# A transformer tower on one core: a new order at two seams, and a hand-written place for every score maximum

## The chip, the core and the metric

The kernel runs on one NeuronCore of a Trainium2 chip. It is one program, launched once. The metric is the device time in microseconds (us): the median of three runs, and beside them one profiled execution whose trace gives every row below. The engines are TensorE (PE, with its weight loads as PEld), VectorE (DVE), ScalarE (ACT), GpSimd (POOL) and SyncE (SP, which issues DMAs). Each engine works through its own list of instructions in order, and waits on semaphores that other engines raise.

## The reference

Two sequences of 2048 tokens, width 128, pass through three layers:

```python
h = take(W.T, x) + b + positional                       # token rows, 128 wide
h = h + attn(layernorm(h))                              # 8 heads of 16, linear in the scores
h = h + ffn(layernorm(h))                               # attention of 2 heads of 64, then experts

# attn: masked q.k, normalised by its running mean and variance, no softmax
dots = where(causal_mask, 0, q @ k.T * scale)
t = dots - mean_so_far;  normed = t * rsqrt(mean_so_far(t*t) + EPS)
out = where(causal_mask, 0, normed * g + b) @ v

# ffn: softmax attention over unit q and k, then 8 experts, all used, mixed by a gate
attn = softmax(where(causal, l2(q) @ l2(k).T * scales, min))
y = (attn @ v) @ Wo
out = sum_e softmax(y @ gate_W + gate_b)[e] * (gelu(y @ W1[e] + b1[e]) @ W2[e] + b2[e])
```

## The kernel before

The tokens are cut into 16 blocks of 128 positions, each with both sequences (B = 2). All engines' orders are written out by hand, one function per engine.

**Stage A, the first attention (0 to about 222 us).** Because that attention has no softmax, it is computed as a recurrence over the blocks: a state (`sg`) is carried, and each block adds its own part. Block 0 is worked by a direct way of its own. In it VectorE makes the masked dots and their variance, GpSimd raises the variance to the power -0.5 (`coefs`, line 268), VectorE copies the new state out of PSUM (`state_out`, line 656) and GpSimd adds it up (`state_add`, line 264). Blocks 1 to 14 run in `step_a(c, nxt)`, one call for each block on each engine. In it PE does the dots of the first sequence (`dots`), sums, the dots of the second, the projections of the next block, and the products with the masked dots. Each block needs its input two steps ahead: `embed(c)` (VectorE: add the position, row statistics), `front(c)` (GpSimd: the statistics' power, lines 251 and 253), `normed(c)` (VectorE, line 648), and PE's transposes `xn_T(c)` (line 1032). For block 2 these stand between block 0 and `step_a(1)`: GpSimd's order is `coefs(0)`, `state_add(0)`, `front(2, 0)`; VectorE's is `state_out(0, 0)`, `state_out(0, 1)`, `embed(2)`, `normed(2)`; PE fills the time with `busy`, matmuls whose result nobody reads.

**The seam to stage B (about 215 to 232 us).** The last block (15) is written out without a loop, mixed with the first blocks of the next stage. PE ends its products with `project2(1)`, which projects block 1 for the second attention and waits until ScalarE has copied block 15's sums out of PSUM (`sums_out`, line 435).

**Stage B (about 232 to 278 us)** makes q, k and v of the second attention: `squares`, `sum_squares`, `l2_factors`, `unit_qk`, a chain of ScalarE, VectorE and GpSimd around PE's transposes. Some of PE's matmuls there (line 1245) also have no reader.

**Stage C, the second attention (about 278 to 486 us).** There are 8 items (4 chunks of 512 queries, 2 sequences), cut into 80 steps of 128 keys each. `plan()` makes the lists. In each step s, in this order on PE: `scores(s)`; a part of the row maxima of a later item; the values of step s - 2; the output part of an earlier item, if one is due at this step; then, where the step has two maxima, the second one. The parts of an output are five matmul groups that come 1, 2, 3, 7 and 8 steps after the step at which that item's output is due (`YAT`). A maximum is a pair of score matmuls into PSUM banks 3 and 4 (`pair_scores`) and a reduction of both by VectorE (`row_max`, line 866). As the two banks are used every time, the next pair waits until VectorE has reduced the one before:

```python
if guard:
    pe.wait_ge(*guard)          # guard = S["sm_used"], k + 1
```

`MSLOT` says which maxima stand in which step. Up to step 8 they come one or two at a time for the small items. From step 9 on a step has one or two ("a double step"). From step 36 (`CLOSE`) on, the last maximum of a step stands after the output part instead of before the values. VectorE's order in a step is: the maxima (both, when there are two), `head_out` if an item ends (lines 941 and 943: it scales the item's values and releases their banks, for which PE's first values of the next item wait), the gate's small operations, and the low halves of the exponentials that are VectorE's share (line 976). GpSimd takes the other low halves (line 384): both of a step, or one where `on_pool` gives the odd one to VectorE, which is in odd steps from 17 to 61 with one maximum.

In the kernel before, `plan()` spreads the maxima by a rule: as many in each step as the items' due steps ask for. This gives double steps at 9, 12, 15, 17, 20, 26, 31, 37 and 42.

**Stage D, the experts (about 486 to 832 us):** 64 rounds of up-projection, gelu, down-projection and weighted sum.

## Time and profile before

| | |
|---|---|
| three runs | 835.01 us median, 833.29 to 840.62 |
| profiled execution | 834.53 us; the span of its trace is 832.7 us, with 1.8 us around it |
| PE busy | 778.6 us (94%) |
| DVE busy | 703.0 us (84%) |
| ACT busy | 486.5 us (58%) |
| POOL busy | 337.3 us (41%) |
| mean granted clock of PE | 0.99 |

A busy share says how long an engine had an instruction in work, not that it worked at its peak: a matmul at half clock is busy twice as long. In the rows below, times count from the span's start. In a row of the timeline the brackets hold the engine's idle time before the instruction and the instruction that ended it. PE's rows are matmuls; the line 1024 is that of the helper `mm`, so they are told apart by tiles and shapes: `ps<-y,room 64x512 f32` is `dots`, `ps<-qh,kh 64x512 f16` begins `scores`, `ps<-v,room 128x65` are the values, `ps<-cst 128x512 f32` is `busy`.

### The profile page before, as it was taken

The page shows a single profiled execution, that of the slowest core. Times are in us where ns is not written, and L with a number is a line of the kernel's source. Part 1 is how long each engine was busy: PE and PEld are TensorE (multiplying, and loading weights), DVE is VectorE, ACT ScalarE, POOL GpSimd, SP SyncE. Part 2 cuts the span into 40 slices and gives each one's busy share as a digit, 9 for nine tenths or more (in the row PEclk, how much of TensorE's full clock was granted, in tenths as well). Part 3 has the DMA queues.
Part 4 walks back from the last instruction along what each step waited for, and adds up shares of the span by engine and source line. Part 5 has one row for each costly group of instructions (what it writes and reads, how often), then busy time and mean ns, then how long its engine had stood idle before and what let it go on. Part 6 is the DMA issues. An engine that isn't in the chain of part 4 may idle for free.

```text
span 832.7 us, 21068 instructions
## 1 busy us (share of the span) xinstructions
PE 778.6 (94%) x8230; PEld 552.5 (66%) x8230; DVE 703.0 (84%) x1575; ACT 486.5 (58%) x1023; POOL 337.3 (41%) x374
## 2 busy tenths in 40 slices
PE   1999999999988889998899999999999999999997
PEld 1568778877755455555556556777777777777775
DVE  3649988999688776777667999999999999999997
ACT  2435555555388667786878767455555555555553
POOL 6638999877575557665766631000000000000000
PEclk9989999999999999999999999999999999999999
DMA  4200111010000000000000000000000000000000
GB/s 132 55 10 20 39 39 27 26 27 14 1 1 1 26 2 2 3 2 2 2 2 3 2 14 2 13 2 14 2 14 2 5 11 9 7 6 11 2 15 13
DMA packets 9666, 12.09 MB, mean 15 GB/s; under 512 B 1856, under 2 KB 6592, under 8 KB 9568
## 3 DMA queue, kind: packets, MB, share of 16 engines
q1 hardware_dynamic: 8544, 8.65, 3.5%
q0 software_dynamic: 1024, 2.10, 0.9%
q8 instruction: 65, 1.06, 0.5%
q14 instruction: 33, 0.27, 0.1%
HBM read 8.65 MB, written 2.10 MB: 13 GB/s over the span
## 4 chain that ended last, share of the span: by engine, by line
PE 75%; DVE 12%; issue 5%; POOL 4%; ACT 3%; DMA 1%; DVEq 0%; ACTq 0%
PE ps L1024 74%; DVE mx L866 2%; POOL ss L345 2%; DVE room L974 2%; DVE room L976 1%; DVE qkn L820 1%; ACT room L592 1%; POOL sm L268 1%; DVE mx L861 1%; DVE ss L805 1%; DMA h_all<-emb_rows,idx 1%; DVE y L701 1%; DVE och L943 1%; PE ps L1032 0%; PE ps L1052 0%
## 5 line engine op out<-in xcount | busy, mean ns | idle before, releaser
L605 ACT ACTIVATE cst<-ps,col 128x512 f32<-128x512 f32 x256 | 175.6, 687 | 157.8 <-PE ps L1024 157.0
L1024 PEld LDWEIGHTS ps<-arena,sq 128*128 128x128 f16 x3072 | 191.9, 98 | 62.0 <-DVE sq L1005 4.9
L1024 PE MATMUL ps<-arena,sq 128*128 128x128 f16 x3072 | 213.1, 219 | 0.3 <-DVE sq L1005 0.2
L1024 PE MATMUL ps<-y,arena 128*128 128x512 f16 x768 | 207.4, 379 | 0.4 <-issue 0.4
L1005 DVE TENSOR_TENSOR sq<-cst,sq 128x512 f16<-128x512 f32 x256 | 176.3, 689 | 4.5
L384 POOL TENSOR_TENSOR room<-room 128x512 f16<-128x512 f32 (+3 forms) x122 | 123.2, 1029 | 74.8 <-ACT room L592 73.9
L999 DVE CAST sq<-cst 128x512 f16<-128x512 f32 x256 | 109.8, 429 | 7.5 <-ACT cst L605 0.5
L583 ACT ACTIVATE room<-ps 128x512 f32<-128x512 f32 (+3 forms) x160 | 76.7, 533 | 43.3 <-PE ps L1024 42.9
L866 DVE TENSOR_REDUCE mx<-ps 128x2 f32<-128x1024 f32 (+2 forms) x64 | 70.2, 1096 | 36.7 <-PE ps L1024 36.5
L1024 PEld LDWEIGHTS ps<-y,arena 128*128 128x128 f16 x768 | 64.5, 98 | 32.0 <-issue 1.2
L992 DVE SCALAR_TENSOR_TENSOR h_all<-ps,gs,h_all 128x128 f32<-128x128 f32 x256 | 77.2, 343 | 0.4 <-PE ps L1024 0.4
L1024 PEld LDWEIGHTS ps<-v,room 128*128 128x128 f16 x1632 | 55.8, 98 | 31.6 <-issue 13.8
L1024 PE MATMUL ps<-v,room 128*128 128x65 f16 (+1 forms) x1632 | 66.2, 195 | 7.7 <-DVE och L943 5.1
L592 ACT CAST room<-room 128x512 f16<-128x512 f32 (+3 forms) x142 | 72.5, 561 | 0.0
L1024 PEld LDWEIGHTS ps<-room,y 128*128 128x128 f32 x512 | 60.9, 192 | 2.7 <-ACT y L467 1.7
L1024 PE MATMUL ps<-room,y 128*128 128x34 f32 (+1 forms) x512 | 60.0, 272 | 0.5 <-ACT y L467 0.5
L268 POOL TENSOR_TENSOR sm<-sm,mhalf 128x16 f32<-128x16 f32 x15 | 43.6, 2908 | 27.5 <-DVE sm L747 22.1
L1024 PE MATMUL ps<-kh,qh 64*128 64x512 f16 (+3 forms) x160 | 33.2, 354 | 10.4 <-DVE mx L866 8.6
L752 DVE TENSOR_TENSOR y<-ps,cst 128x1024 f32<-128x1024 f32 x30 | 36.3, 1211 | 7.5 <-PE ps L1024 7.5
L976 DVE TENSOR_TENSOR room<-room 128x512 f16<-128x512 f32 (+3 forms) x38 | 36.4, 957 | 3.8 <-ACT room L592 3.1
L1024 PE MATMUL ps<-y,room 64*128 64x512 f32 x128 | 39.1, 694 | 0.0
L239 POOL DMA_INDIRECT h_all<-emb_rows,idx x32 | 31.6, 988 | 10.3 <-issue 7.9
(166 smaller groups left out, 1189.5 us busy)
## 6 DMA issues: line engine op xcount, KB each, us to landing
sq<-w_rows SPq DMA_DIRECT2D x13, 256.0 KB, 2.8
out<-h_all SPq DMA_DIRECT2D x32, 64.0 KB, 1.6
cst<-consts SPq DMA_DIRECT2D x1, 896.0 KB, 5.3
h_all<-emb_rows,idx POOLq DMA_INDIRECT x32, 2.6
hxT<-w_rows SPq DMA_DIRECT2D x2, 256.0 KB, 2.7
cst<-consts SPq DMA_DIRECT2D x1, 398.0 KB, 3.7
c<-consts SPq DMA_DIRECT2D x1, 256.0 KB, 5.2
x<-w_rows SPq DMA_DIRECT2D x1, 256.0 KB, 3.0
```

The costliest lines, as they stand in the source:

```text
L268: g.tensor_tensor(sm[:, 4], sm[:, 3], mhalf[:].rearrange("p (b h) -> p b h", b=B), ALU.pow).then_inc(S["r_ready"], 1)
L384: g.tensor_tensor(plo[:, i % PR, lo:], p32[:, i % QR, lo:], phi[:, i % PR, lo:], ALU.subtract).then_inc(S["plo_pool"], 1)
L583: a.activation(p32[:, i % QR, lo:], ps[:, i % 3, lo:], ACT.Exp).then_inc(S["s_used"], 1)
L592: a.copy(phi[:, i % PR, lo:], p32[:, i % QR, lo:]).then_inc(S["p_ready"], 1)
L605: a.activation(hid[:, f], ps[:, HBANK[f], :], ACT.Gelu_apprx_tanh, bias=col[:, K_B1 + k:K_B1 + k + 1], scale=1.0 / WS).then_inc(S["hid_rea ...
L752: v.tensor_tensor(dtm[:, b], ps[:, 3:5, :].rearrange("p z (h j) -> p (z h) j", j=P), upper.unsqueeze(1).to_broadcast([P, HA, P]), ALU.mult ...
L866: v.tensor_reduce(mx[:, it % 2, r, kb], ps[:, 3:5, 0:w], AX, ALU.max).then_inc(S["sm_used"], 1)
L976: v.tensor_tensor(plo[:, i % PR, lo:], p32[:, i % QR, lo:], phi[:, i % PR, lo:], ALU.subtract).then_inc(S["plo_dve"], 1)
L992: v.scalar_tensor_tensor(hr, ps[:, EBANK[n % 2], r * D:(r + 1) * D], gs[:, m, r, n % E:n % E + 1], hr, ALU.mult, ALU.add).then_inc(S["eo_u ...
L999: v.tensor_copy(hhi[:, f], hid[:, f]).then_inc(S["hhi_ready"], 1)
L1005: v.tensor_tensor(hlo[:, f], hid[:, f], hhi[:, f], ALU.subtract).then_inc(S["hlo_even" if f % 2 == 0 else "hlo_odd"], 1)
L1024: return t_.matmul(o, l, r, start=start, stop=stop, skip_group_check=True)
```

## The change

It does three things, and gives the maxima new steps.

1. At the end of block 0, GpSimd's order becomes `front(2, 0)`, `state_add(0)`, `coefs(0)`. VectorE's becomes `state_out(0, 0)`, `embed(2, 0)`, `state_out(0, 1)`, `normed(2, 0)`. The call `busy(1, 1)` ahead of PE's `xn_T(2)` is taken out.
2. At the seam to stage B, three matmuls of 512 columns in half precision, with no reader, are put ahead of `project2(1)`.
3. VectorE does the closing maxima of a step (the second one of a double step up to 35, and the last one from step 36 on) after `head_out` instead of before it. A function `closing(s)` counts them, for PE and VectorE alike; PE's own rule is unchanged.

The maxima follow a written list, `COUNTS`, of how many stand in each step. Their order is unchanged. The double steps from 9 on are now 9, 11, 14, 18, 20, 27, 28, 41 and 45. Each item's last maximum stays at or before its old due step. As `on_pool` looks at the number of maxima, the odd low halves of steps 17, 31 and 37 go to VectorE, and those of steps 27, 41 and 45 go to GpSimd.

```diff
--- before.py
+++ after.py
@@ -315,9 +315,9 @@
             out_bias(0)
             out_bias(1)
             gather(6, 16)
+            front(2, 0)
+            state_add(0)
             coefs(0)
-            state_add(0)
-            front(2, 0)
 
             def step_a(c, nxt, more=2, tail=True):
                 if c >= 3:
@@ -707,8 +707,10 @@
             link(v.tensor_reduce(sm[:, 1, 1], sq[:, 1], AX, ALU.add))
             dve.wait_ge(S["sq_act"], 1)
             v.tensor_scalar(sm[:, 3], sm[:, 1], inv0, DOT_EPS, ALU.mult, ALU.add).then_inc(S["var_ready"], 1)
-            for b in range(B):
-                state_out(0, b, first=True)
+            state_out(0, 0, first=True)
+            embed(2, 0)
+            state_out(0, 1, first=True)
+            normed(2, 0)
 
             def outputs(c, cur, first=False):
                 dve.wait_ge(S["coef"], c + 1 if c < NT - 1 else NT + 1)
@@ -783,8 +785,6 @@
                     normed(c + 2, cur)
                 h1_out(c - 1)
 
-            embed(2, 0)
-            normed(2, 0)
             step_a(1, 0, first=True)
             for c in range(2, NT - 2, 2):
                 for u in range(2):
@@ -951,13 +951,17 @@
                     if s == YAT[m] + DVE_Y[2]:
                         out_part(m, 5)
                 two = MSLOT.get(s, ())
-                for part in two if two and two[0][0] not in ALONE else two[:1]:
+                early = 1 if two and two[0][0] in ALONE else len(two) - closing(s)
+                for part in two[:early]:
                     row_max(*part, (0, 1))
                 if s == 1:
                     low_qk(NT - 1)
                 for it in range(len(ITEMS)):
                     if s == OAT[it]:
                         head_out(it)
+                if two and two[0][0] not in ALONE:
+                    for part in two[early:]:
+                        row_max(*part, (0, 1))
                 for m in range(LAST):
                     if s - YAT[m] in DVE_Y[:2]:
                         out_part(m, DVE_Y.index(s - YAT[m]) + 3)
@@ -1119,7 +1123,6 @@
                     at = D + h * XW + DA
                     last = mm(ps[:, 5 + b, at:at + DA], dtm[:, b, h], kv[0][:, b, h, DA:2 * DA], start=False)
                 last.then_inc(S["x_ps"], 1)
-            busy(1, 1)
             xn_T(2, 0, first=True)
 
             def step_a(c, nxt, more=True, first=False):
@@ -1220,6 +1223,8 @@
                 last.then_inc(S["x_ps"], 1)
                 if b == 0:
                     project2(0, [1])
+            for i in range(3):
+                mm(ps[:, 3, :], minus16, c16[:, 0:CH])
             project2(1)
             out_T(NT - 2)
             normed_T(2)
@@ -1421,10 +1426,10 @@
                 lone = [(*part, h) for part in MSLOT.get(s, ()) if part[0] in ALONE for h in range(HS)]
                 pairs = [part for part in MSLOT.get(s, ()) if part[0] not in ALONE]
                 assert not (lone and pairs)
-                closing = min(len(pairs), 1) if s >= CLOSE else len(pairs) // 2
+                close = closing(s)
                 for part in lone[:1]:
                     lone_scores(*part)
-                for part in pairs[:len(pairs) - closing]:
+                for part in pairs[:len(pairs) - close]:
                     pair_scores(*part)
                 if s in RAT:
                     max_row(RAT[s])
@@ -1439,13 +1444,13 @@
                 for part in lone[2:]:
                     lone_scores(*part)
                 if s < CLOSE:
-                    for part in pairs[len(pairs) - closing:]:
+                    for part in pairs[len(pairs) - close:]:
                         pair_scores(*part)
                 for m in range(LAST):
                     if s - YAT[m] in PE_Y:
                         out_part(m, PE_Y.index(s - YAT[m]) + 1)
                 if s >= CLOSE:
-                    for part in pairs[len(pairs) - closing:]:
+                    for part in pairs[len(pairs) - close:]:
                         pair_scores(*part)
 
 
@@ -1479,6 +1484,8 @@
 
 
 ALONE = (1, 2)
+COUNTS = [int(d) for d in "0222222"
+          "1121211211121211111122111111111111211121111111111111111"]
 
 
 def plan():
@@ -1493,18 +1500,12 @@
                 for r in range(4):
                     parts.append((it, r, kb, CH if kb < c else (r + 1) * P, k))
                     k += HS if it in ALONE else 1
-    due = [None, 2, 6] + [f - 3 for f in first[3:]]
-    mslot, done, credit = {}, 0, 0.0
-    for s in range(1, len(steps)):
-        left = [(sum(p[0] <= it for p in parts) - done, due[it] - s) for it in range(1, len(items)) if due[it] >= s]
-        credit += max((n / (d + 1) for n, d in left), default=0)
-        count = max([int(credit + 1e-6)] + [n - 2 * d for n, d in left])
-        for part in parts[done:done + count]:
-            mslot.setdefault(s, []).append(part)
-        done, credit = done + count, max(credit - count, 0)
+    mslot, done = {}, 0
+    for s, count in enumerate(COUNTS):
+        if count:
+            mslot[s] = parts[done:done + count]
+            done += count
     assert done == len(parts)
-    for it in range(1, len(items)):
-        assert max(s for s, ps in mslot.items() for p in ps if p[0] == it) <= due[it]
     rat = {first[it] - 1: it for it in range(1, len(items))}
     o_at = [e - 1 + LAG for e in first[1:] + [len(steps)]]
     y_at = []
@@ -1540,11 +1541,17 @@
     return {0: 1, 1: 7, 2: 5}.get(c, 0)
 
 
+def closing(s):
+    parts = [part for part in MSLOT.get(s, ()) if part[0] not in ALONE]
+    return min(len(parts), 1) if s >= CLOSE else len(parts) // 2
+
+
 def on_pool(i):
     s = i // 2
     if s >= NSTEP - 18:
         return i % 2 == 0
-    return i % 2 == 0 or len(MSLOT.get(s, ())) != 1 or s < 16 or s % 2 == 0
+    parts = len(MSLOT.get(s, ()))
+    return i % 2 == 0 or s < 16 or parts > 1 or parts == 1 and s % 2 == 0
 
 
 def rounded(i):
```

## Rows read from the trace of the kernel before

**Rows 1.** Windows: busy us (instructions) of five engines, granted clock, DMA, GB/s
```profile
45.00:59.00 14.00, 14.00 (x71) 9.90 (x72) 7.05 (x16) 4.05 (x12) 4.98 (x7) 0.76 0.00 1
216.00:232.00 16.00, 14.79 (x76) 10.04 (x75) 9.40 (x26) 5.24 (x13) 7.17 (x9) 0.89 0.00 1
400.00:490.00 90.00, 82.86 (x1316) 52.68 (x1311) 71.23 (x99) 71.34 (x149) 55.47 (x50) 0.98 0.01 2
516.00:832.00 316.00, 312.10 (x3557) 228.17 (x3554) 300.25 (x715) 160.97 (x235) 0.00 (x0) 1.00 0.03 8
```

**Rows 2.** Timeline, end of block 0: start, us, engine, line, operation
```profile
38.03 2.94 POOL L268 TENSOR_TENSOR sm<-sm,mhalf 128x16 f32<-128x16 f32 x1 [4.68 <-DVE sm L709]
...
41.11 0.43 DVE L631 TENSOR_TENSOR h_all<-h_all,cst 128x256 f32<-128x256 f32 x1
41.19 1.96 PE L1024 MATMUL ps<-room,y 128*128 128x16 f32 x16 [0.47 <-ACT y L467]
...
42.20 0.15 DVE L641 BATCH_NORM_AGGREGATE mv<-st 128x2 f32<-128x6 f32 x1
...
43.00 1.10 PE L1024 MATMUL ps<-cst 128*128 128x512 f32 x2
...
43.58 0.71 POOL L253 TENSOR_TENSOR rs<-rs,mhalf 128x2 f32<-128x2 f32 x1
...
44.98 0.69 PE L1032 MATMUL ps<-cst,room 128*128 128x128 f32 x2 [0.88 <-DVE room L648]
45.60 2.08 PE L1024 MATMUL ps<-y,room 64*128 64x512 f32 x4
...
60.16 1.13 PE L1024 MATMUL ps<-y,room 64*128 64x512 f32 x4
```

**Rows 3.** Chain that ended last: start, us; one merged piece of two consecutive blocks
```profile
59.06 3.79 PE ps L1024 x22
...
70.97 3.79 PE ps L1024 x22
```

**Rows 4.** Timeline, the seam to stage B
```profile
225.86 2.90 PE L1024 MATMUL ps<-wsm,hxT 128*128 128x384 f32 x4 [0.67 <-ACT room L435]
...
230.53 1.49 PE L1024 MATMUL ps<-wsm,hxT 128*128 128x384 f32 x4
...
232.51 1.03 PE L1024 MATMUL ps<-c 128*128 128x512 f16 x4
...
232.57 0.69 DVE L820 TENSOR_TENSOR qkn<-ps,ss 128x512 f32<-128x512 f32 x1 [0.84 <-PE ps L1201]
```

**Rows 5.** Waits in all: engine, line, for whom; us in total, times, longest
```profile
PE ps L1024 <- DVE mx L866: 8.6, 19, 1.2
...
PE ps L1024 <- DVE och L943: 5.1, 5, 1.6
```

**Rows 6.** Timeline of PE: where scores of steps 14 to 17 begin, and transposes
```profile
318.64 0.39 PE L1024 MATMUL ps<-qh,kh 64*128 64x512 f16 x2
...
320.67 0.39 PE L1024 MATMUL ps<-qh,kh 64*128 64x512 f16 x2
...
323.56 0.66 PE L1353 MATMUL ps<-cst,och 128*128 128x128 f32 x4
...
324.15 0.39 PE L1024 MATMUL ps<-qh,kh 64*128 64x512 f16 x2
...
327.23 0.34 PE L1024 MATMUL ps<-qh,kh 64*128 64x384 f16 x2
```

**Rows 7.** Timeline of PE: first values after the items' ends, steps 38, 50
```profile
385.14 0.91 PE L1024 MATMUL ps<-v,room 128*128 128x65 f16 x24 [1.62 <-DVE och L943]
...
416.41 1.15 PE L1024 MATMUL ps<-v,room 128*128 128x65 f16 x24 [1.62 <-DVE och L943]
```

**Rows 8.** Timeline of VectorE: the second maximum of step 17
```profile
330.14 1.22 DVE L866 TENSOR_REDUCE mx<-ps 128x2 f32<-128x1024 f32 x1 [0.49 <-PE ps L1024]
```

**Rows 9.** Costliest groups: busy us, mean ns, idle before
```profile
L976 DVE TENSOR_TENSOR room<-room 128x512 f16<-128x512 f32 (+3 forms) x38 | 36.4, 957 | 3.8 <-ACT room L592 3.1
```

## The prediction

> **What bounds the kernel now.** I read the windows by stage first, to see where PE is not simply at work at full clock. The experts (516 to 832 us) are: busy 312.1 of 316 us at a granted clock of 1.00 [rows 1]. The change doesn't touch them, so a gain ahead of them arrives in full at the end. Three stretches show a lower clock. From 45 to 59 us the mean is 0.76, so 0.24 x 14 / 0.5 = 6.7 us at the lower level (1.2 GHz); from 216 to 232 it is 0.89, so 3.5 us; from 400 to 490 it is 0.98, so 3.6 us [rows 1]. The first two are the change's two seams. Then I read the timeline at each seam, to see what PE waited for before the clock fell, and the chain of waits, to have the length of an undisturbed block. For the second attention I read the table of waits and PE's timeline: there PE works in steps of fixed content, so the distance between the beginnings of two `scores` is the length of a step, and what a double step costs can be read from steps of either kind.
>
> **Part 1, the end of block 0.** Before, GpSimd takes `coefs` first (its power alone is 2.94 us from 38.03), then two state additions, and ends the power of `front(2)` at 43.58 + 0.71 = 44.29. PE has done the last 16 products at 41.19 + 1.96 = 43.15, has filled 43.00 to 44.10 with `busy`, and begins the transposes of block 2 at 44.98, after 0.88 us of idleness ended by VectorE; `dots(1, 0)` begins at 45.60 [rows 2]. After, `embed` (41.11 to 42.35, 1.24 us) stands before the second `state_out`. That one ends just where `embed` begins now, at about 41.1, and waits for PE until then, so VectorE has the time. The rest is an estimate from these rows: `embed` from about 38.4 to 39.7, `front(2)` on GpSimd to about 40.7, `normed` at 41.2 behind the second `state_out`, done by 41.9. PE's own products, until 43.0, are then last, and the transposes follow at once. They took 0.69 at the lower clock, so some 0.4 at full clock: `dots(1, 0)` at about 43.4, **2.2 us earlier**. What is put back: the two state additions by about 1 us (the first begins near 40.7, still before `sums(1, 0)` asks for it near 44.6), and `coefs`, to end near 46 instead of 41.9. VectorE asks for the coefficients in `outputs(0)`, behind two masked dots, that is some 6 us after `dots(1, 0)`, near 49.5. The cover is over 3 us; without it each microsecond would cost one. `busy` costs nothing by going: PE has real work in its place.
>
> Block 1 itself: from `dots(1, 0)` at 45.60 to `dots(2, 0)` at 60.16 it lasts 14.56 us [rows 2], while two undisturbed blocks in the chain lie 70.97 - 59.06 = 11.91 us apart [rows 3]. The same `dots` took 2.08 at the lower clock and 1.13 at full [rows 2]. If PE keeps its clock through the seam, block 1 takes 11.91, and **2.65 us** come back. For this, PE no longer stands idle before the transposes, and dots and sums follow where filler and a pause stood. Sum of part 1: 4.85 us. Its bounds are 2.2 (the clock falls all the same) and 4.85.
>
> What a page says against it stands apart. The trace shows the clock of 45 to 59 us low after a stretch of narrow products, filler and a pause. The Trainium skill ("TensorE: Matmul & The Clock Gate", part 4 on PE-mode transposes) says that transposes don't count as PE being busy in the same way. The change puts transposes where filler stood, so by that rule the clock would fall all the same, which is the second rival's time below.
>
> **Part 2, three matmuls at the seam to stage B.** PE waits 0.67 us before `project2(1)`, for ScalarE's copy of the sums, and then runs its four pieces in 2.90 us, where the same four pieces of the next block take 1.49 [rows 4]. Four 512-column matmuls of the same kind as the new ones take 1.03 us together [rows 4], so three take at most 0.77: 0.67 of that fills the wait, and 0.1 is the most that shows. If they hold the clock, 1.41 comes back, and about 0.2 from the transposes behind. Who is late next: VectorE's `unit_qk(1)` waits 0.84 for PE at 232.57 [rows 4], so at least that much is PE's doing there; the chain of squares and powers also begins with `project2(1)` and moves with it. Bounds 0.8 and 1.6; I take **1.4**, as both feeders move.
>
> **Part 3, the maxima.** In all, PE waits 8.6 us for maxima and 5.1 us for `head_out` [rows 5]. The last is largest at steps 38 and 50, 1.62 us each [rows 7]: there VectorE does a maximum ahead of `head_out`, though the values that `head_out` needs are long done. With `closing`, `head_out` goes first at steps 9, 37 and 49, and both waits of 1.62 lose their cause. At step 9 PE's next pair waits for the same maximum, so nothing comes of it.
>
> Against that stand the new places. Step 14 has one maximum and no output part: 320.67 - 318.64 = 2.03 us. Step 15 has two and the transposes of an output (0.66): 324.15 - 320.67 = 3.48. Step 16 has one and a projection: 327.23 - 324.15 = 3.08 [rows 6]. So beside an output part a second maximum costs 3.48 - 2.03 - 0.66 = 0.8. Alone it must cost more: a pair and the hand-over take 0.49, the reduction 1.22 [rows 8], two rounds of that are 3.42, and 3.42 - 2.03 = 1.4. Five of the seven double steps that are given up (15, 17, 26, 31, 42) hold an output part; the seven new ones (11, 14, 18, 27, 28, 41, 45) hold none of the long ones. That costs 5 x 0.6 = 3.0 us. Some maxima in the new places are narrower, by the plan's list of parts. Scaling 1.22 by columns (an estimate), step 11 has 256 columns less than step 12 had and saves 0.6; step 28 holds one of 128 columns, saving 0.9; step 45 one of 384, saving 0.3. So the places cost 1.2 to 1.3 us. The low halves that change engine (0.96 us each on VectorE [rows 9]) are three each way: nothing in sum, up to 1 us either way by where they fall; at step 17 VectorE's comes ahead of the two maxima of step 18, which is bad.
>
> Of the two waits of 1.62 I keep the one at step 50, since no double step comes behind it. The one at step 38 is followed by the double steps 41 and 45, and at 41 VectorE also has the sum of an output part in front; I count it as given back there. So part 3 comes to 1.3 - 1.62 = **-0.3 us**. Its bounds: -3.2 (both waits, places free) and +3.
>
> **The sum.** The profiled execution took 834.53 us, 832.7 of it in the span; it is 0.5 us under the median of the three runs and inside their spread. 834.53 - 4.85 - 1.4 - 0.3 = **828.0 us**.
>
> **The rivals.** (a) The second attention gains: both waits for `head_out` go for good and the new places cost nothing. For it: 8.6 us of waits for maxima can shrink as well. Against it: the prices above. 834.53 - 6.25 - 3.24 = 825.0 us. (b) The clock falls at both seams all the same, after other instructions. Then only the 2.2 us of the earlier start and part 3 are left: 832.0 us. For it: the 16 narrow products that precede the first seam [rows 2] stay as they are. The rule on transposes above gives this time too. Against it: at the second seam the three matmuls lie exactly in the pause that precedes the fall. (c) Slower than before: a bare double step costs 1.4 us at all seven new places, while the steps that are freed keep their length, because the copies between an output's parts set them and not the maximum. 7 x 1.4 = 9.8, less 4.85 + 1.4 + 1.62 = 7.9: 836.5 us. It decides if the freed steps give back less than 1.9 us together, under 0.3 each. Against it: step 15 with two maxima is 0.8 longer than its single maximum and its transposes explain. (d) The change doesn't do what it says at the seams: GpSimd, 41% busy over all but with a chain of its own in block 1, is late next, and hardly anything arrives: 834 us.
>
> **How the numbers follow.** My forecast has a chance of 0.50, with 1.5 us either way; (a) 0.17, (b) 0.15, (c) 0.10, (d) 0.08. The range of 823 to 834 us takes in the forecast, most of (a), all of (b) and half of (d); it leaves out (c) and the ends, about 0.18. One per cent, which is about what a measurement of this kernel can tell from no change, is 8.35 us: 826.7 and 843.4. Under 826.7 lie most of (a) and a fifth to a quarter of the forecast's own spread, in sum some 0.28 to 0.30; above 843.4 only a larger (c).
>
> **What would show it.** In the changed kernel the transposes of block 2 should begin near 43.0 and `dots(2, 0)` near 55.3, and the clock from 45 to 59 us should be near 1.00. `project2(1)` should take 1.5 us, not 2.9, and the clock from 216 to 232 should be near 1.00 too. The waits for `head_out` should fall from 5.1 to about 2 us. Step 14 should be near 3.4 us, where it was 2.03, and step 15 near 2.7, where it was 3.48. I am wrong if the clock falls at another place of the same stages, if `coefs` turns out late in block 1, or if the waits for maxima grow by more than 3 us.

## The result, and the profile after

The changed kernel takes 832.68 us in the median of 22 runs (829.8 to 838.42), the kernel before, in as many runs beside it, 838.56 us (832.91 to 842.6). The ratio is 0.9947, 95% interval 0.9926 to 0.9968: 4.4 us of 838.56 (2.7 to 6.2), faster, but by less than one per cent. The forecast was 828.0 us. The time lies in the range, in the direction forecast, and 4.7 us above it. One of the six executions of a version further down, the changed kernel with its gathers spread, took 1008.01 us at a granted clock of 0.75, and its ratio leaves it out.

Two numbers of these runs matter below. The median of before is 838.56, not the 835.01 of the three runs shown; its profiled execution, 834.53, falls among the six of the 22 that lie between 832.9 and 835.1, while the other sixteen lie between 837.0 and 842.6. And the profiled execution of the changed kernel, 836.64 us with a span of 834.8, is one of its longer ones. So the two profiles show the kernels from opposite sides of their spreads, and by them alone the change would be a loss. The spread goes with TensorE's mean granted clock: the fifteen executions of the changed kernel at 0.991 or more take 829.8 to 833.83 us, the seven at 0.987 to 0.989 take 834.8 to 838.42.

The windows of the changed kernel, columns as in [rows 1], with a stretch ahead:

```profile
41.00:55.00 14.00, 14.00 (x53) 10.54 (x54) 3.01 (x6) 2.69 (x8) 5.79 (x7) 0.51 0.08 30
...
45.00:59.00 14.00, 14.00 (x58) 9.71 (x56) 6.89 (x16) 2.92 (x11) 6.33 (x8) 0.65 0.00 1
216.00:232.00 16.00, 15.08 (x94) 10.66 (x93) 10.23 (x22) 5.63 (x16) 8.06 (x10) 1.00 0.00 1
```

Against [rows 1]: the seam to stage B has full clock now (0.89 before), the first seam has less than before (0.65, was 0.76), and from 41 to 55 us TensorE worked at its lower level, 1.2 GHz, nearly throughout (0.51).

The timeline of the changed kernel, end of block 0:

```profile
31.90 0.94 PE L1028 MATMUL ps<-wqkv,room 128*128 128x128 f32 x6 [0.36 <-issue]
...
33.15 0.95 POOL L239 DMA_INDIRECT h_all<-emb_rows,idx  x1 [0.30 <-issue]
...
35.90 0.37 ACT L421 COPY room<-ps 128x256 f32<-128x256 f32 x1 [4.05 <-remote]
...
39.97 2.58 PE L1028 MATMUL ps<-room,y 128*128 128x16 f32 x16 [3.01 <-ACT y L467]
...
45.50 3.60 PE L1028 MATMUL ps<-room,y 128*128 128x16 f32 x16
48.94 0.67 PE L1036 MATMUL ps<-cst,room 128*128 128x128 f32 x2
49.53 2.08 PE L1028 MATMUL ps<-y,room 64*128 64x512 f32 x4
...
63.68 1.13 PE L1028 MATMUL ps<-y,room 64*128 64x512 f32 x4
```

and the chain of waits there, just ahead of that copy at 35.90:

```profile
31.84 4.03 another core or an unknown queue
```

Read them together. TensorE's six products for the second sample of block 1 end at 32.84. The copy on ScalarE that waits for nothing but them (line 421) begins at 35.90, 3.06 us later. The profile can't name who released it ("remote"), and the chain calls the 4 us before it an unknown queue, on a kernel of one core. Everything behind that copy is late by as much: the squares, the copy of the differences (line 467), and TensorE's narrow products at 39.97, before which it stood idle for 3.01 us. Then the clock falls, at 41.1, and stays low until 54.8. In the profile of before the same copy waited 1.02 us, and TensorE went from filler to narrow products without a pause:

```profile
33.08 0.37 ACT L421 COPY room<-ps 128x256 f32<-128x256 f32 x1 [1.02 <-PE ps L1024]
...
34.44 2.74 PE L1024 MATMUL ps<-cst 128*128 128x512 f32 x6
...
37.16 1.96 PE L1024 MATMUL ps<-room,y 128*128 128x16 f32 x16
```

The rest of the reordering is as drawn: the transposes (48.94) follow the last narrow products at once, where 0.88 us of waiting and `busy` stood [rows 2], and `dots(1, 0)` (49.53) follows the transposes.

The seam to stage B, against [rows 4]:

```profile
229.38 1.53 PE L1028 MATMUL ps<-wsm,hxT 128*128 128x384 f32 x4
...
234.72 0.69 DVE L820 TENSOR_TENSOR qkn<-ps,ss 128x512 f32<-128x512 f32 x1 [0.84 <-PE ps L1204]
```

`project2(1)` takes 1.53 us instead of 2.90 and its wait of 0.67 is filled. VectorE's wait of 0.84 stays.

TensorE's waits in all, against [rows 5]:

```profile
PE ps L1028 <- DVE mx L866: 12.9, 20, 1.6
...
PE ps L1028 <- DVE och L943: 1.3, 2, 1.1
```

`head_out` is waited for 1.3 us instead of 5.1, maxima 12.9 instead of 8.6: 14.2 in place of 13.7. And the timeline of TensorE where the scores of steps 14 to 22 begin, against [rows 6]:

```profile
319.92 0.39 PE L1028 MATMUL ps<-qh,kh 64*128 64x512 f16 x2
...
322.72 0.38 PE L1028 MATMUL ps<-qh,kh 64*128 64x512 f16 x2
...
324.21 0.39 PE L1028 MATMUL ps<-kh,qh 64*128 64x512 f16 x2 [0.46 <-DVE mx L866]
...
326.19 0.39 PE L1028 MATMUL ps<-qh,kh 64*128 64x512 f16 x2
...
329.27 0.34 PE L1028 MATMUL ps<-qh,kh 64*128 64x384 f16 x2
...
332.06 0.28 PE L1028 MATMUL ps<-qh,kh 64*128 64x256 f16 x2
...
335.45 0.39 PE L1028 MATMUL ps<-kh,qh 64*128 64x512 f16 x2 [1.60 <-DVE mx L866]
...
337.17 0.23 PE L1028 MATMUL ps<-kh,qh 64*128 64x128 f16 x2 [0.99 <-DVE mx L866]
...
338.10 0.61 PE L1028 MATMUL ps<-qh,kh 64*128 64x512 f16 x2
...
343.66 0.39 PE L1028 MATMUL ps<-qh,kh 64*128 64x512 f16 x2
```

VectorE ahead of the maxima of step 18:

```profile
333.71 0.55 DVE L980 TENSOR_TENSOR room<-room 128x384 f16<-128x384 f32 x1
334.18 1.21 DVE L866 TENSOR_REDUCE mx<-ps 128x2 f32<-128x1024 f32 x1
```

Step 14 lasts 2.80 us (was 2.03), step 15 3.47 (was 3.48), step 16 3.08 as before. Step 15 has lost a maximum and is no shorter: its one pair (324.21) waits 0.46 us for VectorE, which still has the second maximum of step 14. In the double step 18, VectorE first does step 17's low half, which GpSimd did before (0.55 us from 333.71), and reduces the first maximum from 334.18. TensorE waits 1.60 and 0.99 us for maxima, and then the product that takes 0.38 to 0.39 in the other steps takes 0.61: here too it is at the lower clock, this time in the middle of the second attention.

### The profile page after: what moved, and what is told of

The parts are those of the page before. It is cut to its first block, busy times and chain, and to the rows that moved or that the text cites. A ratio compares the mean times of both kernels' runs of the same rounds, so it can differ in the third digit from the quotient of the medians.

```text
span 834.8 us, 21070 instructions
## 1 busy us (share of the span) xinstructions
PE 779.2 (93%) x8231; PEld 553.8 (66%) x8231; DVE 703.8 (84%) x1575; ACT 487.3 (58%) x1023; POOL 337.6 (40%) x374
## 4 chain that ended last, share of the span: by engine, by line
PE 76%; DVE 12%; issue 5%; ACT 3%; POOL 3%; DMA 1%; another core or an unknown queue 0%; DVEq 0%; ACTq 0%; POOLq 0%
PE ps L1028 74%; DVE mx L866 3%; POOL ss L345 2%; DVE room L978 2%; DVE room L980 1%; DVE qkn L820 1%; DMA h_all<-emb_rows,idx 1%; ACT room L592 1%; DVE mx L861 1%; DVE ss L805 1%; PE ps L1036 0%; PE ps L1056 0%; DVE och L943 0%; POOL sm L282 0%
## 5 line engine op out<-in xcount | busy, mean ns | idle before, releaser
L1028 PEld LDWEIGHTS ps<-room,y 128*128 128x128 f32 x512 | 63.1, 198 | 5.4 <-ACT y L467 4.4
L1028 PE MATMUL ps<-room,y 128*128 128x34 f32 (+1 forms) x512 | 62.3, 277 | 3.0 <-ACT y L467 3.0
L1028 PE MATMUL ps<-kh,qh 64*128 64x512 f16 (+3 forms) x160 | 33.2, 355 | 14.7 <-DVE mx L866 12.9
```

The source lines that it names most:

```text
L1028: return t_.matmul(o, l, r, start=start, stop=stop, skip_group_check=True)
```

## The experiments

Comparisons are with the kernel before on the same chip. Its medians there were 837.17 (runs 1 to 4), 838.39 (5 to 8), 837.16 (9 to 11) and 836.03 (12).

### Each part alone

Part 1 alone, the end of block 0:

```diff
-            coefs(0)
-            state_add(0)
+            front(2, 0)
+            state_add(0)
+            coefs(0)
...
-                state_out(0, b, first=True)
+            state_out(0, 0, first=True)
+            embed(2, 0)
+            state_out(0, 1, first=True)
+            normed(2, 0)
...
-                    busy(1, 1)
```

> Part 1 alone: the new order at the end of block 0 and no filler there, everything else as before. Theory 1 (the prediction's sum): the transposes of block 2 follow PE's products without a pause, the clock holds, and the median falls by 4.85 us, to about 0.994 of before. Theory 2 (the clock falls all the same, because a stall of ScalarE earlier in block 0 leaves PE without work, as in the profile of the changed kernel, where a copy began after 4.05 us of idle time): only the earlier start is left, 2 us or less, 0.998, and the granted clock of the stretch from 45 to 59 us stays well under 1.

Measured: 834.12 us, ratio 0.9955 (0.9927 to 0.9982), so 3.8 us where T1 said 4.85 and T2 2 or less; the interval (1.5 to 6.1 us) holds both. Its profile, of the shortest of its twelve executions, 829.34 us, shows the seam at its best, with a clock of 1.00 from 45 to 59 us as T1 had it; timeline:

```profile
36.15 3.59 PE L1024 MATMUL ps<-room,y 128*128 128x16 f32 x16 [2.86 <-ACT y L467]
...
42.69 1.96 PE L1024 MATMUL ps<-room,y 128*128 128x16 f32 x16
...
44.84 1.13 PE L1024 MATMUL ps<-y,room 64*128 64x512 f32 x4
...
56.53 1.13 PE L1024 MATMUL ps<-y,room 64*128 64x512 f32 x4
```

TensorE had waited 2.86 us here too and was at the lower clock at 36.15, but it was back before the seam: the second narrow products take 1.96, and both `dots` 1.13. From the second narrow products to `dots(2, 0)` it is 56.53 - 42.69 = 13.84 us. In before it was 60.16 - 41.19 = 18.97 [rows 2], in the profile of the changed kernel 63.68 - 45.50 = 18.18. This distance contains nothing but the seam and block 1 and is the measure of part 1 from here on.

Part 2 alone, `for i in range(3): mm(ps[:, 3, :], minus16, c16[:, 0:CH])` ahead of `project2(1)`:

> Part 2 alone: the three matmuls ahead of project2(1). Theory 1: the clock from 216 to 232 us is 1.00, the four pieces of project2(1) take 1.5 us and the median falls by 1.4 us (0.998). Rival: the clock falls a little later instead, or the chain of GpSimd's powers sets the stage, and nothing is measured (1.000).

Measured: 836.86 us, ratio 0.9992 (0.9965 to 1.002): between 2.9 us and a loss of 1.7, unclear. In its profile `project2(1)` runs at full clock (1.53 us), and yet the window of 216 to 232 has 0.89 as in before; timeline and windows:

```profile
231.73 1.53 PE L1024 MATMUL ps<-wsm,hxT 128*128 128x384 f32 x4
```

```profile
216.00:232.00 16.00, 15.53 (x96) 11.99 (x95) 9.36 (x19) 5.24 (x14) 8.37 (x10) 0.89 0.00 1
```

The clock is low in an earlier part of that window, from 218.2 to 221.8 us. The rival has the fall move as well, but to a later place.

Part 3 alone, the list `COUNTS` and `closing` (the diff stands above):

> Part 3 alone: head_out before the closing maxima, and the new places. Theory 1: the second attention (scores of step 0 to scores of step 62) is 0.3 us shorter, 1.000 in the median; steps 14, 18 and 28 near 3.4 us. Rival (a) of the prediction: 3.2 us shorter, 0.996. Rival (c): some 8 us longer, 1.010.

Measured: 837.3 us, ratio 0.9994 (0.9964 to 1.0024): neither a gain nor a loss that the times can show, and not rival (c). The steps show more, in profiles that keep full clock there: from the scores of step 0 to those of step 62, TensorE takes 165.21 us with the attention of before (part 2 alone) and 165.40 with part 3 (the filler's run below), 0.2 longer. In the profile of this run it is 166.90, as the clock falls behind step 18 again. The three parts alone sum up to 3.8 + 0.7 + 0.5 = 5.0 us, near the 4.4 of all three together, but each is uncertain by 2.3 to 2.5 us, so whether they act on each other is not shown.

The seams and `head_out` first, with the old places of the maxima (the cut shows it against the changed kernel):

```diff
-COUNTS = [int(d) for d in "0222222"
-          "1121211211121211111122111111111111211121111111111111111"]
...
+    due = [None, 2, 6] + [f - 3 for f in first[3:]]
...
```

> The whole change without the new places: seams and head_out first, the double steps where they were (9, 12, 15, 17, 20, 26, 31, 37, 42). If the new places cost what the prediction says (1.3 us) and the wait for head_out at step 38 is only given back by the double steps 41 and 45, this kernel is 1.3 to 2.9 us faster than the changed one: 0.990 to 0.992 of before if the changed kernel is at 0.9947. If the new places gain, it is slower than the changed one.

Measured: 829.19 us, ratio 0.9889 (0.9857 to 0.9921), faster than the changed kernel by 0.0058 x 837 = 4.9 us. The new places cost more than the 1.3 us of the prediction, or the 2.9 if the wait at step 38 is theirs too. Timeline of TensorE, scores of steps 17 and 22:

```profile
329.71 0.34 PE L1028 MATMUL ps<-qh,kh 64*128 64x384 f16 x2
...
341.62 0.39 PE L1028 MATMUL ps<-qh,kh 64*128 64x512 f16 x2
```

Steps 17 to 21 take 341.62 - 329.71 = 11.91 us; in the changed kernel 343.66 - 329.27 = 14.39.

### What in part 3 gains and what costs

`head_out` first and nothing else, against the kernel before:

```diff
-                for part in two if two and two[0][0] not in ALONE else two[:1]:
+                early = 1 if two and two[0][0] in ALONE else len(two) - closing(s)
+                for part in two[:early]:
                     row_max(*part, (0, 1))
...
                         head_out(it)
+                if two and two[0][0] not in ALONE:
+                    for part in two[early:]:
+                        row_max(*part, (0, 1))
```

> Edit: the kernel before with head_out in front of the closing maxima alone; places and seams as before. T1 (the nine new places, not head_out, are what makes the third part worth nothing: with head_out first and the old places the trace of the earlier run was 4.36 us ahead of the kernel before between the first second-attention step and step 62, with the new places 0.09): the waits for head_out at steps 38 and 50 both go, steps 0 to 62 take about 4.3 us less than in the profile of before (1.5 of it only because the lower clock at 416.89 is gone, 2.8 without), ratio to before 0.995 to 0.9965. T2 (the prediction's: of the two waits of 1.62 one is lost later on): 1.6 us less, ratio 0.998. The maxima at 18 are at 17 here, so no granted clock under 1.00 between steps 17 and 21.

Measured: 834.68 us, ratio 0.997 (0.994 to 0.9999). Waits of TensorE:

```profile
PE ps L1028 <- DVE mx L866: 9.8, 21, 1.2
...
PE ps L1028 <- DVE och L943: 1.1, 1, 1.1
```

10.9 us in place of the 13.7 of before [rows 5]: 2.8 us less, both waits of 1.62 gone for good. That is T1 by the waits, and by the steps: 0 to 62 take 162.33 us, 2.9 less than the 165.21 of before's attention at full clock. The time, 2.5 us (0.1 to 5.0), agrees with T1 and doesn't exclude T2's 1.6.

One place put back, the second maximum of step 18 in step 17:

```diff
-          "1121211211121211111122111111111111211121111111111111111"]
+          "1121211211211211111122111111111111211121111111111111111"]
```

> Edit: the changed kernel with one of the nine places put back: the second maximum of step 18 in step 17 again. T1 (this one move is the dear one: between steps 16 and 21 the changed kernel is 2.49 us behind the old places, because the double at 18 lets TensorE wait 1.60 and 0.99 us for maxima and its clock then falls from 338.07 to 341.48): steps 16 to 21 take 2.3 to 2.8 us less than in the changed kernel, no clock under 1.00 there, ratio to before 0.9947 - 0.003 = 0.9917. T2 (every new place costs about the same, 4.3/7 = 0.6 us): 0.6 us less, ratio 0.994, and the lower clock at 338 stays.

Measured: 832.96 us, ratio 0.9937 (0.9906 to 0.9967): nearer to T2's 0.994, with T1's 0.9917 in the interval. In its profile steps 17 to 21 take 11.91 us at full clock, 2.48 less than in the changed kernel, as T1 had it; here the clock falls in steps 10 and 11 (low from 308.6 to 312.1 us). The waits for maxima fall to 11.5 us (12.9 in the changed kernel), 1.4 less, so the 2.49 us of T1 are not what the move costs each time: see the filler's run below, with the same places, where the clock did not fall in these steps.

All old places but 12, which goes to 11:

```diff
-          "1121211211121211111122111111111111211121111111111111111"]
+          "1121211121211211111211112111112111121111111111111111111"]
```

> Edit: the changed kernel with the old places except one, 12 moved to 11 as in the changed kernel. T1 (that move is the only one of the seven that gains: steps 11 and 12 take 4.57 in the changed kernel against 4.87): 0.3 us less than with all old places, ratio to before 0.9885. T2 (the 0.3 is given back at step 14, where the items' due times are): the same as with all old places, 0.989. Either way faster than the changed kernel by 4 to 5 us.

Measured: 830.36 us, ratio 0.990 (0.9857 to 0.9942). The waits of TensorE for maxima are 9.4 us here and 9.8 with all old places, and steps 0 to 62 take 161.73 us here and 162.37 there. That is T1 in the steps, by 0.6 us instead of 0.3; so small a difference the times can't show (0.990 against 0.9889).

### The late signals

Six instead of three `busy` products while TensorE waits for ScalarE in block 0:

```diff
-                    busy(1, 3)
+                    busy(1, 6)
```

> Edit: the changed kernel with six instead of three filler products (each two records of 512 columns) behind the transposes of block 0, while TensorE waits for ScalarE's copy. T1 (the clock falls at 41.11 us in the profile because TensorE stands 3.0 us idle before the narrow products, which in turn is because the signals of the products that ended at 32.83 to 34.39 us arrived only at 35.88 to 36.03): the fillers cover that wait at no cost, the granted clock of 41 to 55 us rises from 0.51 to over 0.8, the time falls by 3 to 6 us, ratio to before 0.988 to 0.991. T2 (the narrow products and transposes behind the wait bring the clock down, filler or not, and the fillers make executions without late signals 2.6 us later): clock 41 to 55 still 0.5 to 0.65, ratio 0.995 to 0.998.

Measured: 832.66 us, ratio 0.9932 (0.9906 to 0.9957). Timeline and windows:

```profile
40.63 1.96 PE L1028 MATMUL ps<-room,y 128*128 128x16 f32 x16 [1.44 <-ACT y L467]
45.45 2.19 PE L1028 MATMUL ps<-room,y 128*128 128x16 f32 x16
47.84 1.13 PE L1028 MATMUL ps<-y,room 64*128 64x512 f32 x4
...
59.53 1.13 PE L1028 MATMUL ps<-y,room 64*128 64x512 f32 x4
...
326.49 0.34 PE L1028 MATMUL ps<-qh,kh 64*128 64x384 f16 x2
...
339.70 0.39 PE L1028 MATMUL ps<-qh,kh 64*128 64x512 f16 x2
```

```profile
41.00:55.00 14.00, 14.00 (x85) 11.02 (x84) 7.25 (x21) 3.54 (x11) 8.06 (x12) 0.88 0.11 38
```

In the profile T1 comes true: the wait before the narrow products is 1.44 us instead of 3.01, the clock of 41 to 55 us is 0.88 instead of 0.51, and the seam takes 59.53 - 45.45 = 14.08 us instead of 18.18. The clock still falls, but later and for less: it is low from 42.5 to 46.0 us, where it was low from 41.1 to 54.8. So in this execution less idleness before the narrow products went with a shorter fall. The time decides nothing: by the two ratios the filler brings 1.3 us against the changed kernel (0.9932 and 0.9947), less than either interval's half width, and neither T1's 0.988 to 0.991 nor T2's 0.995 to 0.998 holds the ratio. The last two rows answer the question of the run before: with the same places, and without a low clock there, steps 17 to 21 take 13.21 us. The double at 18 costs 13.21 - 11.91 = 1.3 us; the other 1.2 of the 2.49 were the clock, in that execution. The same double steps lost the clock in two profiles (the changed kernel and part 3 alone) and kept it in two (this one, and the changed kernel with the gathers spread, 13.23 us).

What holds the signals? In the profile of the changed kernel GpSimd has issued ten gathers in a row, the last at 33.15, when ScalarE's copy hangs. The gathers were moved out of block 0:

```diff
-            gather(6, 16)
+            gather(6, 8)
...
-                if 16 + 2 * c <= T:
-                    gather(14 + 2 * c, 16 + 2 * c)
+                if 8 + 2 * c <= T:
+                    gather(6 + 2 * c, 8 + 2 * c)
```

> Edit: the changed kernel; GpSimd issues two instead of ten gathers (indirect DMAs) before block 1, and the other eight two at a time at the ends of the steps from block 1 on. In the profiles of all kernels but that of before, signals of TensorE that are due at 29.6 to 34.4 us arrive together at 34.0 to 36.7, 0.2 to 2 us after the tenth gather in a row has been issued. T1 (the gathers in a row hold the signals back): no signal over 0.5 us late, ScalarE's copy of the second sample of block 1 starts within 1.5 us of the one before it, the clock of 41 to 55 us is over 0.9, the times lie closer together, and the median falls by 3 to 4 us: ratio to before 0.990 to 0.991. T2 (the gathers have nothing to do with it): the same late signals at about 35 us, ratio 0.9935 to 0.9947.

Measured: 827.46 us, ratio 0.9884 (0.985 to 0.9919). Timeline and windows:

```profile
30.59 0.37 ACT L421 COPY room<-ps 128x256 f32<-128x256 f32 x1 [1.02 <-PE ps L1028]
...
38.70 1.96 PE L1028 MATMUL ps<-room,y 128*128 128x16 f32 x16 [0.47 <-ACT y L467]
40.51 0.42 PE L1036 MATMUL ps<-cst,room 128*128 128x128 f32 x2
40.85 2.08 PE L1028 MATMUL ps<-y,room 64*128 64x512 f32 x4
...
54.13 1.13 PE L1028 MATMUL ps<-y,room 64*128 64x512 f32 x4
```

```profile
41.00:55.00 14.00, 14.00 (x82) 10.33 (x82) 7.29 (x17) 5.72 (x18) 8.29 (x11) 0.88 0.04 10
...
45.00:59.00 14.00, 14.00 (x91) 10.87 (x91) 9.64 (x28) 6.51 (x18) 6.73 (x8) 1.00 0.04 11
```

The copy waits 1.02 us, and for TensorE by name. T1 holds, in the time by more than it said (5 us); the clock of 41 to 55 us, 0.88, is just short of its 0.9. Nothing is late here, and yet the clock falls at 40.8 us, in the transposes, and is low until 44.3: `dots(1, 0)` takes 2.08.

The same with the best places, and with the kernel before:

> Edit: the version with all old places but 12 to 11 (ratio 0.990 alone), with the gathers spread. T1: both gains add up, ratio to before 0.985 to 0.987, 826 to 827 us. T2: as without spreading, 0.990.

Measured: 825.07 us, ratio 0.9856 (0.9826 to 0.9885): T1, with a time 1 us under its range. This version beats the kernel before by 12.1 us, and the changed kernel, by the two ratios, by 0.0091 x 838 = 7.6.

> Edit: the kernel before with the gathers spread alone. T1: the profile shown for before, the only one without late signals, becomes the rule: median 833 to 835 us, ratio 0.995 to 0.996, and the changed kernel with the same edit is then 6 us faster than this one, as the prediction had it against that profile. T2: ratio 1.000, spread of the times as before (832 to 842).

Measured: 832.15 us, ratio 0.9934 (0.9911 to 0.9957): T1, slightly better than it. The changed kernel with the same edit is 4.7 us faster than this, not 6. The times don't lie together as T1 has it: they run from 829.46 to 836.14 us, and the longest is the profiled one, with no signal late and a mean clock of 0.986. Timeline and windows:

```profile
40.77 1.96 PE L1024 MATMUL ps<-room,y 128*128 128x16 f32 x16 [0.47 <-ACT y L467]
45.47 2.08 PE L1024 MATMUL ps<-y,room 64*128 64x512 f32 x4
...
59.27 1.13 PE L1024 MATMUL ps<-y,room 64*128 64x512 f32 x4
```

```profile
45.00:59.00 14.00, 14.00 (x79) 10.46 (x80) 6.86 (x16) 4.55 (x14) 5.73 (x7) 0.83 0.02 5
```

This is the seam of before, out of the late signals' way: 59.27 - 40.77 = 18.50 us, and 54.13 - 38.70 = 15.43 in the changed kernel above.

The two seams without part 3, gathers spread:

> Edit: the kernel before with both seams of the change (parts 1 and 2) and the gathers spread; maxima and head_out as before. Beside it stand the kernel before with the gathers spread (832.15 us, ratio 0.9934) and the changed kernel with them spread (827.46, 0.9884). T1 (parts 1 and 2 carry the change, part 3 nets nothing: its profiles without a lower clock in steps 0 to 62 give +0.2 us): 827.3 us or less, ratio 0.988 to 0.9885, the first second-attention step starts at 271 to 273 us. T2 (part 3 carries a share, as the rival with a gain in the attention has it, 1 us or more): 828.5 to 829.5 us, ratio 0.990 to 0.991. T3 (the prediction's 6.25 us for the seams holds in full against 832.15): 825.9 us, ratio 0.986, and part 3 then costs 1.5 us.

Measured: 829.03 us, ratio 0.9915 (0.9883 to 0.9947): T2's time, its ratio just missed. But T1's 0.9885 is in the interval too, and the intervals of this run and of the changed kernel with the gathers spread (0.985 to 0.9919) overlap, so that part 3 gains 1 us or more there is not shown. The steps say that it doesn't: 0 to 62 take 165.24 us here and 165.47 there. That the seams give less than 6.25 us is shown: 832.15 - 829.03 = 3.1 by the times, 1.6 by the ratios, which are from two chips.

## Why the prediction was wrong

**The base.** The step that failed first is the sum's own starting point: "The profiled execution took 834.53 us ... it is 0.5 us under the median of the three runs and inside their spread". Three runs can't tell a median from an end. 838.56 - 834.53 = 4.0 of the 4.7 us by which the forecast was too low are here; the change itself was forecast at 6.5 and is 4.4 by the ratio (2.7 to 6.2), 5.9 by the medians. What the trace of that execution lacks is the late signals in block 0. In all nine other profiles of kernels with ten gathers in a row ScalarE stands idle in that place for 2.5 to 5.1 us, at one of the two copies or both; in all four with the gathers spread for 1.02 or 1.03; and spreading them takes the kernel before from 837.16 to 832.15, under its profiled execution, and the changed kernel from a ratio of 0.9947 to 0.9884. How much of the 4.0 us they are is not shown: only profiled executions show them, and the granted clock parts executions too. The one profiled with the gathers spread and nothing else has no signal late and took 836.14, and part 1 alone took 829.34 with signals late.

**Part 1.** The order of work is right. From the narrow products to `dots(1, 0)` it was 45.60 - 41.19 = 4.41 us [rows 2]; with the gathers spread it is 40.85 - 38.70 = 2.15 in the changed kernel: 2.26 earlier, and 2.2 was forecast. `coefs` was not late: in the changed kernel it ends at 50.79 us, and VectorE takes it up at 57.70. The mis-sized term is the clock's, "If PE keeps its clock through the seam, block 1 takes 11.91, and **2.65 us** come back". In all nine profiles with part 1 the clock falls once between 35 and 43 us, and what comes back depends on where. In three it falls ahead of the second narrow products (at 35.5, 35.6 and 42.5 us) and is back before these or soon after their start: 13.84 (one place put back), 13.84 (part 1 alone) and 14.08 us (filler) from the second narrow products to `dots(2, 0)`, for a forecast of 18.97 - 4.85 = 14.12. In the three with the gathers spread, the seam as the prediction drew it with nothing late and no pause before the transposes, it falls at 40.5 to 41.1 us, during or just behind the transposes: 15.42 to 15.47. Block 1 then takes 13.13 to 13.32 us instead of 11.91, so 1.2 to 1.4 of the 2.65 come back. In the other three (the changed kernel, and all or nearly all old places) the clock is low through the whole seam: 18.18 to 18.24. The mean of the nine is 15.9; that of the five without part 1 is 18.8 (18.50 to 18.99). So part 1 is worth 2.9 us of the 4.85 in these profiles, and 3.8 (1.5 to 6.1) in the time.

This is rival (b) at the first seam, in six profiles of nine: the clock is low there all the same. Which instructions bring it down is not shown. In the profile of the changed kernel it is low from 41.1 us, in the narrow products behind TensorE's idleness; the transposes come at 48.94. In the profile of part 1 alone the transposes lie between 42.69 and 44.84, and the clock stays full behind them. In the changed kernel with the gathers spread the fall comes in the transposes (40.51 to 40.93, the clock low from 40.8), with the narrow products just ahead. The rule of the Trainium skill weighed in the prediction ("TensorE: Matmul & The Clock Gate", part 4) is that transposes don't count as the array being busy in the same way. By the three profiles with the gathers spread it may have a part in the fall, by part 1 alone two transposes don't suffice for one, and no run here parts them from the narrow products.

**Part 2.** The mechanism is right in every profile: `project2(1)` takes 1.53 us in all nine that have the three matmuls, against 2.90, 2.90, 2.64 and 2.67 in four of the five that don't. The term of 1.4 leaves out two things. In the fifth without them (part 1 alone) the clock was full there anyway, 1.53. And in five of the nine with them the clock is low for a while in the 20 us ahead of it (a mean of 0.89 to 0.91 over 16 us), as where part 2 stood alone; the last sentence of the prediction named this, "the clock falls at another place of the same stages".

**Part 3.** Its sum, -0.3 us, stands against 0.9994 (a gain of 0.5, uncertain by 2.5), against waits that go from 13.7 to 14.2, and against steps 0 to 62 that take 0.2 us longer at full clock. It is near only because two steps of it are wrong in opposite directions. "The one at step 38 ... I count it as given back there" failed: `head_out` first takes 2.8 us of waits, 2.9 of the steps and 2.5 of time (0.1 to 5.0) away, not 1.62, and steps 40 to 43 take 11.60 us in the changed kernel, 11.53 with the old places. "So the places cost 1.2 to 1.3 us" failed too: 14.2 - 10.9 = 3.3 us of waits, and 165.40 - 162.33 = 3.1 us of the steps. The prediction's own sign for being wrong, waits for maxima that grow by more than 3 us, came true (12.9 - 8.6 = 4.3).

Step by step, between those two profiles (the filler's, and `head_out` first alone), the seven steps that lost a maximum are 6.6 us shorter together; the prediction's prices make 5 x 0.8 + 2 x 1.4 = 6.8. The seven that gained one are 8.6 longer, where 7 x 1.4 less the narrower maxima, 1.8, makes 8.0. And the steps between, which the prediction leaves as they are, are 1.0 longer in sum, step 39 by 0.86 and step 19 by 0.52. So what was wrong is to price each step by itself. A maximum too many is paid in part in the next step, as in step 15, which should have shrunk to 2.7 us and stayed at 3.47 because its pair waits for step 14's second maximum, while step 14 rose to 2.80 and not to 3.4. And the moved low half was put at nothing in sum, though the text calls its place at step 17 bad: there it lies ahead of the maxima of step 18, and moving the one maximum from 17 to 18 costs 1.3 us, not 0.6. Rival (c), that the freed steps keep their length, is true of step 15 alone, and for another reason than its own (the wait for VectorE, not the copies between the output's parts). Rival (a), that the attention gains, needs the old places: 0.9889.

What stays open: by what way the gathers hold up signals between other engines, whether by being issued or by the data that they move; why the late signals are missing in the profile of before, which has the same ten gathers in a row; how much of the 5 us of spreading them is the delay and how much the clock behind it; and what brings the clock down at the first seam.

## What to carry to other kernels

Take the base of a sum from many runs, and see by time and granted clock where among them the profiled execution lies before pricing anything: here 4 us were lost on that, with a change forecast at 6.5. Read a schedule's price from the distance over all its steps, not from single ones: a wait moves on into the next step. A copy that waits for "remote" on a one-core kernel is a question, not a detail: look at what the other engines issue at that moment, and try moving it. And two edits that cancel (`head_out` first, new places) look like one that does nothing, so time each alone.

## What the runs showed of the hardware

Ten gathers in a row on GpSimd (in the changed kernel 0.94 to 1.04 us each and 0.30 apart) lie beside signals between TensorE and ScalarE that arrive late, in the changed kernel by 3 us (32.84 to 35.90), in nine profiles of ten. Two in a row, with the others two at a time in later steps, show no such delay in four profiles, and are worth 5 us of time. The order of the other work is the same.

TensorE's clock falls at different places in different profiles. At the first seam it was low from 41.1 to 54.8 us in the changed kernel, and from 40.8 to 44.3 with the gathers spread. It can also fall in the middle of a stage whose steps otherwise repeat to 0.02 us (step 16: 3.07 or 3.08 in eleven profiles), as behind the waits of 1.60 and 0.99 us at step 18: steps 17 to 21 took 14.39 and 14.71 us in two profiles with that double step, 13.21 and 13.23 in two others.
